# Where VectorE prepares its constants, and by what route the last two chunks' activation is turned, in a state-space block with a ternary feed-forward

## The reference

```python
x = x + attn(layernorm(x))     # "attn" is a gated state-space block
x = x + ffn(layernorm(x))

def attn(u):                   # 512 inner channels, 8 heads, state 16
    zxbcdt = u @ W_in.T
    xBC = silu(causal_conv4(xBC) + conv_b);  dt = softplus(dt + dt_bias)
    h = exp(dt * A) * h + dt * x (outer) B;  y = h . C + D * x      # scan over positions
    y = layernorm(y) * ln_gamma + ln_beta
    y = sigmoid(y @ W_gate.T + b_gate) * y
    return concat([silu(z0) * x0, y]) @ W_out.T

def ffn(x):                    # 256 -> 1024 -> 256, weights rounded to -1, 0, 1
    h = gelu(x @ absmean(W_fc))
    h = layernorm(h) * ln_w + ln_b
    return h @ absmean(W_proj)
```

## Time and profile before

| | us |
|---|---|
| median of 3 runs | 1085.3 |
| lowest, highest | 1080.65, 1086.47 |
| the profiled execution: its own time | 1079.52 |
| the profiled execution: span of the instructions | 1077.5 |
| TensorE busy (share of the span) | 1024.1 (95%) |
| VectorE busy | 937.5 (87%) |
| ScalarE busy | 921.2 (85%) |
| GpSimd busy | 499.8 (46%) |

### The profile page before, as it was taken

The page is one execution under the profiler, slowest core; times in us unless marked ns, Lnnn a source line. Parts: engine busy times, 40 slices in busy tenths (PEclk is TensorE's granted clock), DMA queues, the critical chain, the costliest instruction groups (busy, mean ns, idle before and its releaser), DMA issues.

```text
span 1077.5 us, 29342 instructions
## 1 busy us (share of the span) xinstructions
PE 1024.1 (95%) x11438; PEld 654.7 (61%) x11438; DVE 937.5 (87%) x1976; ACT 921.2 (85%) x1626; POOL 499.8 (46%) x590
## 2 busy tenths in 40 slices
PE   4879998989999999999999999999999999999997
PEld 2444755657575665757566675756657575766674
DVE  5999996979899998898998999997998989878675
ACT  4978687988889898999889998998879888898775
POOL 1535453444645355355544555355444444543642
PEclk9788999999999999999999999999999999999999
DMA  8312432644645473464656365353564345363758
GB/s 295 81 32 61 82 73 50 110 71 99 111 91 92 97 129 72 107 113 94 91 97 107 84 115 105 91 108 71 100 101 100 70 100 91 83 107 61 127 114 159
DMA packets 303657, 106.17 MB, mean 99 GB/s; under 512 B 271904, under 2 KB 299808, under 8 KB 303520
## 3 DMA queue, kind: packets, MB, share of 16 engines
q1 hardware_dynamic: 303520, 104.31, 49.5%
HBM read 28.38 MB, written 8.91 MB: 35 GB/s over the span
## 4 chain that ended last, share of the span: by engine, by line
PE 83%; DVE 7%; issue 3%; ACT 3%; DMA 1%; SPq 1%; POOL 0%; DVEq 0%; ACTq 0%; POOLq 0%
PE bank L413 48%; PE bank L665 10%; PE bank L677 9%; PE bank L605 4%; PE bank L614 2%; PE bank L586 2%; PE bank L519 2%; PE bank L560 1%; DVE cv L1079 1%; PE bank L483 1%; PE bank L573 1%; DMA hT<-hb 1%; SPq L1519 1%; DVE st L1034 1%; ACT L182 0%
## 5 line engine op out<-in xcount | busy, mean ns | idle before, releaser
L413 PE MATMUL bank<-xnT,win 128*128 128x512 f16 x1152 | 282.0, 388 | 4.5 <-DVE Xd L1141 3.2
L182 ACT ACT_TABLE_LOAD x147 | 188.6, 1283 | 3.3 <-PEq L1587 0.7
L413 PEld LDWEIGHTS bank<-xnT,win 128*128 128x128 f16 x1152 | 109.9, 100 | 127.3 <-issue 12.9
L413 PE MATMUL bank<-yhl,wg 128*128 128x512 f16 x768 | 174.6, 379 | 0.3 <-DVE cv L1079 0.2
L1079 DVE SCALAR_TENSOR_TENSOR cv<-bank,cws,cv 128x511 f32<-128x511 f32 (+2 forms) x192 | 142.7, 745 | 5.0 <-ACT tail L782 0.5
L1389 POOL TENSOR_TENSOR cat<-sz,cat 128x512 f16<-128x512 f32 x64 | 78.9, 1235 | 131.8 <-ACT cat L900 131.7
L1385 POOL TENSOR_TENSOR caty<-tg,caty 128x512 f16<-128x512 f32 x64 | 83.1, 1299 | 122.6 <-ACT caty L888 122.6
L665 PE MATMUL bank<-wfc,x3T 128*128 128x512 f16 x512 | 129.6, 380 | 0.2
L677 PE MATMUL bank<-wpj,hT 128*128 128x256 f16 x1024 | 123.6, 275 | 4.9 <-DMA hT<-hb 4.9
L413 PEld LDWEIGHTS bank<-yhl,wg 128*128 128x128 f16 x768 | 73.6, 98 | 89.3 <-issue 2.5
L677 PEld LDWEIGHTS bank<-wpj,hT 128*128 128x128 f16 x1024 | 99.7, 98 | 27.1 <-issue 5.3
(11 more groups left out here) (165 smaller groups left out, 2050.6 us busy)
## 6 DMA issues: line engine op xcount, KB each, us to landing
x<-in_x SPq DMA_DIRECT2D x31, 512.0 KB, 4.3
out_y<-x SPq DMA_DIRECT2D x15, 512.0 KB, 3.1
crep<-c_rows SPq DMA_DIRECT2D x16, 256.0 KB
hT<-hb SPq DMA_TRANSPOSE x128, 3.2
caty<-in_wg SPq DMA_DIRECT2D x1, 1024.0 KB, 8.8
x<-in_wout SPq DMA_DIRECT2D x1, 1024.0 KB, 9.8
hT<-in_wfc SPq DMA_DIRECT2D x1, 1024.0 KB, 9.6
hb<-in_wpj SPq DMA_DIRECT2D x1, 1024.0 KB, 11.3
```

What stands on the lines that cost most here:

```text
L182: self.eng.preload_act_table_set(self.table)
L413: m = eng.matmul(b, lhs(p, k), rhs(q, k), start=(n == 0), stop=(n == len(seq) - 1))
```

## The change

The semaphore `powers` is raised behind the six memsets, and GpSimd's `norm_x` waits for it in place of `consts`. The cast and the scalings that need loads become a step `K` of VectorE's order, behind both steps `a0`.

For chunks 2 and 3 of block 15, the high and low halves of `h`, and the four DMA transposes that turn them, go. TensorE turns the float32 `h` itself (`H`, four 128x128 transposes for half a chunk into one PSUM bank), ScalarE evicts the float16 high half into `hT` (`J`), VectorE subtracts it from the bank to get the low half (`J`), and so twice a chunk. The same bank is used for both halves of a chunk and then for its product.

```diff
@@ PE_ORDER, its end
-    "fe7 fe3 fe5 fe2 of4 of1 of6 of0 pe7 ff3 ff5 ff2 pe4 ff1 pe6 ff0 ff3 pe7 ff5 ff2 pf1 pf4 pf6 pf0 "
+    "fe7 fe3 fe5 fe2 of4 of1 of6 of0 pe7 ff3 ff5 ff2 pe4 ff1 pe6 ff0 ff3 pe7 ff5 ff2 pf1 pf4 Hf6 Hf6 pf6 Hf0 Hf0 "
+    "pf0 "
@@ ACT_ORDER, its end
-    "gf mf je qf gf gf jf mf qf gf gf mf jf qf gf gf mf jf qf jf "
+    "gf mf je qf gf gf jf mf qf gf gf mf jf qf gf gf mf Jf Jf qf Jf Jf "
@@ DVE_ORDER, its start and its end
-    "a0 a0 h0 W0 h0 W0 c0 a1 u0 00 N0 20 c0 40 c0 c0 c0 50 Z0 c1 a2 x0 G0 u1 60 c1 x0 g0 x0 01 b0 21 e0 x0 c1 c1 "
+    "a0 a0 K0 h0 W0 h0 W0 c0 a1 u0 00 N0 20 c0 40 c0 c0 c0 50 Z0 c1 a2 x0 G0 u1 60 c1 x0 g0 x0 01 b0 21 e0 x0 c1 "
...
-    "jf pe if jf if pe qf jf if pf jf qf qf pf pf pf "
+    "qf jf pe if jf if pe qf Jf Jf if pf Jf Jf qf qf pf pf pf "
@@ SP_ORDER, its end
-    "je je Xf Xf Xf je je Xf je je jf jf jf jf pe jf jf jf jf pf pf pf pf "
+    "je je Xf Xf Xf je je Xf je je jf jf jf jf pe pf pf pf pf "
@@ TensorE
+            def turn_h(i, n, at):
+                c, half = H_TURNED + n // 2, n % 2
+                b = take(at)
+                pe.wait_ge(ld_const, 16)
+                pe.wait_ge(hn, 4 * i + c + 1)
+                for k in range(4):
+                    m = eng.transpose(b[:, k * P:(k + 1) * P], h[:, (4 * i + c) % 3, half * T + k * P:half * T + k * P + P],
+                                      ident)
+                m.then_inc(h_mm, 1)
+                gives(at, hT_lo, n + 1)
@@ proj
-                pe.wait_ge(ht_hi[buf], 16 * turn)
-                pe.wait_ge(ht_lo[buf], 16 * turn)
+                if i == LAST and c >= H_TURNED:
+                    pe.wait_ge(hT_lo, 2 * (c - H_TURNED) + 2)
+                else:
+                    pe.wait_ge(ht_hi[buf], 16 * turn)
+                    pe.wait_ge(ht_lo[buf], 16 * turn)
@@ ScalarE
+            def turned_hi(i, n):
+                (b,) = bank["H", i, n]
+                c, half = H_TURNED + n // 2, n % 2
+                act.wait_ge(h_mm, n + 1)
+                act.wait_ge(proj_mm, 4 * i + c - 1)
+                if n == 0:
+                    act.wait_ge(ht_hi[0], 16 * (2 * i + (H_TURNED + 1) // 2))
+                    act.wait_ge(ht_hi[1], 16 * (2 * i + H_TURNED // 2))
+                eng.activation(hT[:, c % 2, 0, 4 * half:4 * half + 4, :], b[:, :].rearrange("p (k t) -> p k t", k=4),
+                               ACT.Copy).then_inc(hT_hi, 1)
@@ VectorE
-            eng.memset(mhalf[:, :], -0.5)
-            dve.wait_ge(ld_ul, 16)
...
+            eng.memset(mhalf[:, :], -0.5).then_inc(powers, 1)
+
+            def constants(i, n):
+                dve.wait_ge(ld_ul, 16)
+                eng.tensor_copy(ul[:, :, :], ulf)
+                dve.wait_ge(ld_small, 16)
...
+            def turned_lo(i, n):
+                (b,) = bank["H", i, n]
+                c, half = H_TURNED + n // 2, n % 2
+                ks = slice(4 * half, 4 * half + 4)
+                dve.wait_ge(hT_hi, n + 1)
+                eng.tensor_tensor(hT[:, c % 2, 1, ks, :], b[:, :].rearrange("p (k t) -> p k t", k=4), hT[:, c % 2, 0, ks, :],
+                                  ALU.subtract).then_inc(hT_lo, 1)
@@ GpSimd, norm_x
-                pool.wait_ge(consts, 1)
+                pool.wait_ge(powers, 1)
```

More of the change, by code:

```diff
@@ L217, in build @@
                              "x0t_mm").split())
-        gate_mm, z_mm, x0_mm, out_mm, fc_mm, proj_mm, ones_mm, csum_mm, r0_mm = (
-            sem(n) for n in "gate_mm z_mm x0_mm out_mm fc_mm proj_mm ones_mm csum_mm r0_mm".split())
+        h_mm, gate_mm, z_mm, x0_mm, out_mm, fc_mm, proj_mm, ones_mm, csum_mm, r0_mm = (
+            sem(n) for n in "h_mm gate_mm z_mm x0_mm out_mm fc_mm proj_mm ones_mm csum_mm r0_mm".split())
         a_step, bt_act, xn, xn_hi, conv_ev, bc_act, xs, dt_exp, dt_ln, cum_hi, cum_lo, ec_exp, es_exp, e_exp = (
             sem(n) for n in "a_step bt_act xn xn_hi conv_ev bc_act xs dt_exp dt_ln cum_hi cum_lo ec_exp es_exp e_exp".split())
-        yn, yf_ev, y_hi, tanh, yg_hi, z_silu, cat_hi, gelu, h_mu, h_sq, hn_hi, x2_hi = (
-            sem(n) for n in "yn yf_ev y_hi tanh yg_hi z_silu cat_hi gelu h_mu h_sq hn_hi x2_hi".split())
+        yn, yf_ev, y_hi, tanh, yg_hi, z_silu, cat_hi, gelu, h_mu, h_sq, hn_hi, hT_hi, x2_hi = (
+            sem(n) for n in "yn yf_ev y_hi tanh yg_hi z_silu cat_hi gelu h_mu h_sq hn_hi hT_hi x2_hi".split())
         win_hi, an_exp, wg_hi, wout_hi, w_abs, bhl_hi = (sem(n) for n in "win_hi an_exp wg_hi wout_hi w_abs bhl_hi".split())
[L227 to L230, removed]
+        v_step, consts, powers, x_var, xn_lo, taps, u_cp, dt_min, dt_one, a_hl, cum_rest, seg_l, xd, ce, be, gm = (
+            sem(n) for n in "v_step consts powers x_var xn_lo taps u_cp dt_min dt_one a_hl cum_rest seg_l xd ce be gm".split())
+        s_done, em, y_out, y_var, y_lo, yg, sx, x2_out, x2_var, x2_lo, hn, h_var, hn_lo, hT_lo, x_out = (
+            sem(n) for n in "s_done em y_out y_var y_lo yg sx x2_out x2_var x2_lo hn h_var hn_lo hT_lo x_out".split())
         win_lo, aneg_v, wg_lo, wout_lo, gam_v, wq, bhl_v, r0_v, bgh_v = (
@@ L352, in build @@
         LAST = NBLK - 1
+        H_TURNED = 2
         def part(i, n, halved):
@@ L380, in x2_steps @@
             return i + 1 if i < LAST else i + n + 1
-        LATE = {(LAST - 1, 1): 0, (LAST - 1, 3): 0, (LAST, 1): 0, (LAST, 2): 2}
+        LATE = {(LAST - 1, 1): 0, (LAST - 1, 3): 0, (LAST, 1): 0}
         def h_halves(i, c):
@@ L683, in _ @@
                      "e": grow, "s": suffix, "g": gram, "t": states, "q": seg, "r": carried, "w": own,
-                     "y": turn_y, "G": gate, "z": skip_z, "v": skip_x, "o": out, "f": fc, "p": proj}
+                     "y": turn_y, "G": gate, "z": skip_z, "v": skip_x, "o": out, "f": fc, "H": turn_h, "p": proj}
             for letter, i, n, at in steps_of(PE_ORDER):
@@ L951, in _ @@
                      "t": tanh_g, "k": half_yg, "z": silu_z, "l": half_cat, "g": gelu_h, "m": mean_h, "q": square_h,
-                     "j": half_h, "x": half_x2}
+                     "j": half_h, "J": turned_hi, "x": half_x2}
             for letter, i, n, _ in steps_of(ACT_ORDER):
@@ L971, in _ @@
             eng.memset(mone[:, :], -1.0)
-            eng.memset(mhalf[:, :], -0.5)
-            dve.wait_ge(ld_ul, 16)
-            eng.tensor_copy(ul[:, :, :], ulf)
-            dve.wait_ge(ld_small, 16)
-            eng.tensor_scalar(cws[:, :, :], sm("cw").rearrange("p (j k) -> p j k", j=5), 1.0 / SW, None, ALU.mult)
-            eng.memset(gsw[:, 4:5], SW)
-            eng.memset(gsw[:, 5:6], SW / 2)
-            eng.tensor_scalar(gsw[:, 0:4], sm("lng"), SW, None, ALU.mult)
-            eng.tensor_scalar(bgh[:, :], sm("bg"), 0.5, None, ALU.mult).then_inc(consts, 1)
+            eng.memset(mhalf[:, :], -0.5).then_inc(powers, 1)
[3 more added lines that the diff above has]
+                dve.wait_ge(ld_small, 16)
+                eng.tensor_scalar(cws[:, :, :], sm("cw").rearrange("p (j k) -> p j k", j=5), 1.0 / SW, None, ALU.mult)
+                eng.memset(gsw[:, 4:5], SW)
+                eng.memset(gsw[:, 5:6], SW / 2)
+                eng.tensor_scalar(gsw[:, 0:4], sm("lng"), SW, None, ALU.mult)
+                eng.tensor_scalar(bgh[:, :], sm("bg"), 0.5, None, ALU.mult).then_inc(consts, 1)
             def rest(dst, src, s, hi):
@@ L1280, in add_ffn @@
                                          ALU.add).then_inc(x_out, 1)
-            STEPS = {"W": weights_in, "N": minus_a, "H": thresholds, "T": ternary,
+            STEPS = {"K": constants, "W": weights_in, "N": minus_a, "H": thresholds, "T": ternary,
                      "C": centre, "R": bias_out, "G": bias_gate, "a": var_x, "h": rest_x, "c": tap, "u": copy_u,
@@ L1286, in _ @@
                      "y": var_y, "n": rest_y, "k": gate_y, "v": skip, "o": add_x, "X": rest_x2, "V": var_x2,
-                     "i": centre_h, "q": var_h, "j": rest_h, "p": add_ffn}
+                     "i": centre_h, "q": var_h, "j": rest_h, "J": turned_lo, "p": add_ffn}
             for letter, i, n, _ in steps_of(DVE_ORDER):
```

## The result

The changed kernel's median is 1089.21 us against 1082.33 for the kernel before on the same chip, 19 runs each. The ratio is 1.0056 with a 95% interval of 1.0033 to 1.0079. That is 6.1 us lost, between 3.6 and 8.5. The profiled execution has 1088.84 us, its span is 1086.7.

The account below looks back on a forecast made before the run. TensorE, busy 95% of the span, was taken to bound the kernel, so only the two ends could matter. 8.5 us lost at the end less 0.2 gained at the start made 8.3 lost: median 1093.6, range 1085.5 to 1098.0.

Parts of the forecast that it names:

- The start: Program start: moving the constants brings the first statistics 2.29 us earlier, but only 0.2 is gained.
- the load behind L703: At the start, ScalarE's second weight pair waits for a load landing at 11.84, so none of the 2.29 arrives.
- The 0.2 for block 1's `x`: At the start, SyncE's load of block 1's `x` comes earlier; of VectorE's 0.43 wait, 0.2 us is gained.
- the start comes through: Rival, chance 0.08: the load does not hold the start, which gives 2.7; 5.8 us lost, 1091.1.
- The rounds: At the end, four rounds of transposes and evictions stand in line: first 2.29 at full level, other three 8.40 at half.
- The handovers: At the end, each step between engines takes 0.14 us, the middle of 0.04 and 0.24; three per round.
- The products: At the end, chunk 2's product runs at full level in 1.91 us, chunk 3's at half in 3.41.
- The level should fall again: At the end, TensorE has 1.20 of transposes in 4.6 us between products, so its clock level drops as before.
- The lower bound of 6.0: End's loss with all at full level: GpSimd is last, its variances behind chunk 3's low halves; 6.0 us lost.
- Full level throughout: Rival, chance 0.13: the end's gaps are short enough to keep TensorE at full level; 5.8 us lost, 1091.1.
- half level throughout: Rival, chance 0.17: the end's transposes keep TensorE's level down all the way; 10.3 us lost, 1095.6.
- The rounds overlap: Rival, chance 0.06: at the end, a chunk's second half is turned while the first is evicted; 2.4 us lost, 1087.7.

Follow-up runs that it names:

- e2: The changed kernel with the constants put back ahead of the first statistics, so the end's part alone: ratio 1.0040, median 1087.31 us against the kernel before.
- e1: The kernel before with only the start's part of the change, the moved constants: ratio 1.0018, median 1084.09 us.
- e6: The kernel before with the moved constants, and ScalarE splitting `x` before its second weight pair: ratio 1.0009, median 1081.70 us.
- e7: e6, with SyncE's load of block 1's `x` also moved ahead of the load of `W_out`: ratio 0.9982 against the kernel before, median 1081.19 us.
- e8: The changed kernel unaltered, profiled once more: 1087.52 us, end 16.82.
- e3: The changed kernel with a bank of its own for each second half of chunks 2 and 3: ratio 1.0010 against the kernel before, median 1083.45 us.
- e5: The changed kernel turning chunks 2 and 3 one product earlier, two banks each, square and variances moved earlier: ratio 0.9978 against the kernel before, median 1079.79 us.
- e9: The changed kernel with e5's edits at the end and the start orders of e6 and e7: ratio 0.9940 against the kernel before, median 1075.46 us.
- the filler: The changed kernel with six unread matmuls behind each group of four transposes: ratio 1.0046 against the kernel before, median 1087.75 us, end 14.15.

## Why the forecast held, and where its terms were off

The forecast was 1093.6, a range of 1085.5 to 1098.0, and "slower by over 0.5%" at 0.65. The median is 1089.21 and the loss 0.56%, at the edge of what can be told apart. The direction is shown, and so is the mechanism of the rounds in one line. The size, 8.3, was 2.2 too large (6.1, of 3.6 to 8.5). The runs behind the 6.1 can be of two kinds, whose ends lost 7.25 (the changed kernel) and 4.74 (e2) in the traces, and the forecast had one kind only. Of the 4.4 between 1093.6 and 1089.21, 3.0 is the base: the median before was 1085.3 in three runs and 1082.33 in nineteen. That the sum of the end came as near as it did is in part luck: its rounds were 2.66 too long and its products 1.45 too short.

**The start, forecast 0.2 gained, with the load behind L703 as what is late next.** Right as a mechanism: the row at L719 now names the load, and e1 alone measures no gain. The 0.2 for block 1's `x` failed. I took it that a load issued earlier lands earlier; SyncE's issue grew from 1.49 to 2.93 and the landing stayed at 21.5. e6 and e7 show that it is the load's place behind that of `W_out`. The rival "the start comes through" fell with e1.

**The rounds, forecast 10.69 for four.** They took 4.10 (1076.54 to 1080.64) for chunk 3 and 3.93 (1069.21 to 1073.14) for chunk 2: 8.03. Three terms of mine were off. The handovers were 0.02 to 0.05, not 0.14: twelve of them make some 1.3. I had three rounds at half level and all four were at full or near it, another 1.5. And the first group's transposes began beside the end of chunk 1's product, so that 0.45 of them lay behind it in the chain. The late rows' 0.60 for four was the right row; the start's 1.11 was not. I had put the 1.11 down to the lower level, but over the first 24 us of the kernel before the granted clock reads 1.00, and the only groups at these ends that began under a granted 0.50 stood beside the end of chunk 2's product (0.83 in the changed kernel, 1.00 in e8), so what such a group costs by itself is not known.

**The products, forecast 1.91 + 3.41 = 5.32.** They took 3.40 + 3.37 = 6.77. "The level should fall again" was right, but it fell for both products and, but for 0.4, not in the rounds. So the step that failed is the choice of pieces that run at half level: 1.45 too little in the products, 1.5 too much in the rounds. I had read the earlier trace rows as a level that falls in the gap; those rows show 1.00 through the gap and 0.54 in the work behind it. The changed kernel does just that at chunk 2; at chunk 3 the level fell 0.4 ahead of the product.

Together 8.03 + 6.77 = 14.80 against my 16.01, which puts the end at 7.25 lost in place of 8.5. The lower bound of 6.0 was too high: e2, with both products short, lost 4.74 (14.22 - 9.48), since GpSimd's variances come as much earlier as the rounds are shorter.

**The signs.** Those of the start were all seen: 3.49 for the statistics, 6.17 for the first normalisation, 11.57 with idle time for the second weight pair, 16.97 for the convolution. The last addition came 9.24 later in place of 8.5. At the end two signs were off. The groups of one chunk stood 2.01 and 2.23 apart in place of 2.3 to 2.8, and chunk 2's product began 3.93 behind the end of chunk 1's in place of 4.6 to 5.6: both by the shorter rounds. And the granted clock between the two was 1.00, not under it: the term that put three rounds at half level.

**The rivals.** "Full level throughout" describes e2, so it is a case that the same code takes in some executions; "half level throughout" was never seen in the rounds. "The rounds overlap" fell for the changed kernel, whose halves stand 2.01 apart (1069.05, 1071.06), and was then built as e3: 1.0010. I had it at 1087.7, which is 1.0022 on the base of the prediction.

**The rule for transposes.** The Trainium skill, "VectorE: DVE Perf Modes", section "The three transpose paths", has TensorE at 390 ns a 128x128 bfloat16 block against 1309 by DMA. The traces agree that TensorE's are cheap (here float32 blocks, four in 0.60). They do not bear out the DMA figure as a price per block: in the kernel before, the transpose of a whole 128x1024 half, eight such blocks, took 3.40 from issue to landing (start, us, what):

```profile
1065.90 3.40 DMA hT<-hb
```

Taken as a rule for this edit the comparison failed in the changed kernel, and it held in the traces of e5 and e9, where the evictions it does not count lie under a product. The prediction called an end that loses 2.6 the most that these figures could give; in e5 it came out 3.54 ahead of the DMA route.

The largest part of the loss is thus shown by undoing it: with both products short, the two banks take the end from 14.22 (e2) to 11.28 (e3), and the place, together with the banks and the order around it (e5), takes it below the kernel before. Why the two products run at half level in some executions and not in others of the same code stays open; long products were seen only behind or between such open gaps, in five of eight executions against none of five.

## What to carry to other kernels

A faster route for a transfer pays only where its round trip through other engines has something to lie under: ask what TensorE does between the transpose and the product that needs it, and if the answer is "nothing", move the step ahead by one product and give each half its own bank before judging the route. When the chain names one releaser, look up the landing times of the loads that the step also waits for: here the next gate stood 0.02 behind the first, and a third behind that. In these traces a product that followed a thin stretch took up to 1.8 times its time, and closing the gap did more than filling it: with the filler the end was 14.15, no shorter than the 14.22 of e2 with open gaps at full level, and with the second bank it was 11.28. Ask also whether something waits behind the product anyway: in the old end a product 1.5 longer moved the last addition by 0.2 (9.48 against 9.28).

## What the runs showed of the hardware that was not expected

- SyncE's issue of the same 512 KB load took 1.49 when issued at 13.02, 2.93 to 3.40 at 11.49 to 11.58 (the changed kernel, e1, e3, e5, e6), and 0.38 at 11.59 when it stood ahead of the load of `W_out` instead of behind it (e7). Issued 1.5 earlier behind that load, it landed no earlier (21.49 in the changed kernel). Ahead of it, the statistics that wait for it began at 19.11.
- The granted clock read 1.00 through 4.10 us with 1.31 of transposes and 0.54 in the dense product right behind them, so the row to look at is the one after the gap. The same 16 matmuls took 1.92 (e2) or 3.40 in different executions of one code.
- At the start the granted clock does not tell the speed. In the kernel before, six matmuls of 512 columns took 0.45 each and a little later ten took 0.22 each, and the granted clock read 1.00 over the whole 24 us (two rows of the chain, then a stretch as above):

```profile
18.70 2.71 PE bank L413 x6
...
21.88 2.16 PE bank L413 x10
...
0.00:24.00 24.00, 8.98 (x40) 4.94 (x41) 11.72 (x43) 8.46 (x15) 2.67 (x11) 1.00 0.92 303
```

- The step from one engine to the next, where the waiting engine stood ready, was 0.02 to 0.05 us in the chain of the end; the 0.24 of the earlier trace rows, from VectorE to TensorE too, was not seen there.
